# Placing zero rows, sums, first tokens and expert outputs differently in a graph transformer layer on one core

## What is computed

```python
x = x + gnn(xn, src, dst, edge_attr_20, edge_weight, edge_attr_3) + linear_attention_block(xn)
x = x + moe(layernorm(x))
# gnn: 40,000 edges from idx_j to idx_i
h   = softplus(f_ij @ Wf1 + bf1) - log 2
W   = (h @ Wf2 + bf2) * rcut_ij[:, None]
agg = segment_sum(message(xn[idx_j], direction of r_ij, W), idx_i, 1250)   # 8 x 128 numbers a node
# moe: 8 experts, hidden 1024, each token goes to its best two
out = sum over e of dense_w[:, e] * ((silu(z @ w_gate[e]) * (z @ w_up[e])) @ w_down[e])
```

## Time and profile before

| | before |
|---|---|
| three runs, median | 1680.25 us (1678.17 to 1683.88) |
| the profiled execution, its own time | 1677.54 us |
| its span in the profile | 1675.8 us |
| mean granted TensorE clock | 0.927 of full speed |
| busy: PE, DVE, ACT, POOL | 1448.5, 852.4, 636.9, 759.3 us |
| front block | 0 to about 452 us (last record scatter), next block's first work at 463.2 us |
| edge block | to about 1027 us |
| block of the sums | 1033.7 to 1069.5 us |
| node block | to about 1134 us |
| expert block | to 1675.8 us |

### The profile page before, as it was taken

How to read it: one execution, slowest core, us unless ns; L and a number is a source line. 1 busy time by engine, 2 the same in 40 slices (tenths; PEclk the granted TensorE clock), 3 DMA queues, 4 the chain that set the end, 5 groups by cost and what they waited for, 6 DMA issues and landing times. The chain is left out here.

```text
span 1675.8 us, 29431 instructions
## 1 busy us (share of the span) xinstructions
PE 1448.5 (86%) x8631; PEld 893.0 (53%) x8632; DVE 852.4 (51%) x1980; ACT 636.9 (38%) x1191; POOL 759.3 (45%) x783
## 2 busy tenths in 40 slices
PE   6466998777369999999999996678999999999995
PEld 3243454344124444444444443377787877887784
DVE  7745665577437777777777776452111111111111
ACT  2354555544226666666666664420100110000010
POOL 4577777777635655556565562006211111111111
PEclk7787999898679999999999998777999999999998
DMA  6665333332268888888888888531154252354113
GB/s 260 223 203 157 112 115 115 117 115 106 84 185 246 250 249 248 251 244 251 242 253 251 247 243 231 195 113 19 25 176 144 56 175 79 121 172 172 20 24 80
DMA packets 130911, 275.35 MB, mean 164 GB/s; under 512 B 21286, under 2 KB 68090, under 8 KB 129906
## 3 DMA queue, kind: packets, MB, share of 16 engines
q0 software_dynamic: 50432, 151.03, 30.5%
q1 hardware_dynamic: 80354, 121.25, 21.8%
q10 hardware_dynamic: 80, 2.56, 0.5%
HBM read 211.81 MB, written 65.50 MB: 165 GB/s over the span
## 5 line engine op out<-in xcount | busy, mean ns | idle before, releaser
L1048 POOL DMA_INDIRECT shared<-node_table,shared x343 | 324.2, 945 | 245.5 <-DVE msg L1116 144.6
L1608 PEld LDWEIGHTS psum<-zT,shared 128*128 128x128 f32 x2944 | 349.9, 193 | 66.6 <-issue 64.1
L1608 PE MATMUL psum<-zT,shared 128*128 128x128 f32 x2944 | 353.9, 276 | 9.1 <-issue 5.8
L394 POOL DMA_INDIRECT edge_list<-rec,place x313 | 311.4, 995 | 108.8 <-issue 94.7
L1118 DVE TENSOR_TENSOR msg<-shared,psum 128x768 f32<-128x768 f32 x339 | 321.2, 948 | 0.0
L1144 PE MATMUL psum<-wf,hT 128*128 128x512 f32 x678 | 315.3, 608 | 3.9 <-ACT psum L1080 3.9
L1080 ACT COPY psum<-bias 128x512 f32<-128x512 f32 x343 | 202.1, 590 | 194.6 <-DVE msg L1118 187.6
L1626 ACT ACTIVATE sg<-psum 128x128 f32<-128x128 f32 x184 | 51.0, 277 | 466.7 <-PE psum L1608 466.7
L1116 DVE TENSOR_TENSOR msg<-shared,psum 128x256 f32<-128x256 f32 x339 | 141.0, 416 | 148.9 <-PE psum L1144 147.4
L1672 DVE TENSOR_TENSOR hid<-sg,psum 128x128 f32<-128x128 f32 x184 | 52.6, 286 | 321.4 <-ACT sg L1626 321.4
L1144 PEld LDWEIGHTS psum<-wf,hT 128*128 128x128 f32 x678 | 122.3, 190 | 162.4 <-issue 144.0
(11 more groups left out here) (278 smaller groups left out, 1486.1 us busy)
## 6 DMA issues: line engine op xcount, KB each, us to landing
shared<-edge_list SPq DMA_DIRECT2D x356, 130.0 KB
shared<-in_L_ffn_w_gate SPq DMA_DIRECT2D x8, 2048.0 KB, 9.4
shared<-in_L_ffn_w_up SPq DMA_DIRECT2D x8, 2048.0 KB, 14.3
shared<-in_L_ffn_w_down SPq DMA_DIRECT2D x8, 2048.0 KB, 18.9
shared<-node_table,shared POOLq DMA_INDIRECT x343, 3.7
edge_list<-rec,place POOLq DMA_INDIRECT x313, 2.6
raw<-in_records SPq DMA_DIRECT2D x19, 256.0 KB, 3.5
xrow<-in_x SPq DMA_DIRECT2D x10, 250.0 KB
```

The source lines that it names most:

```text
L394: nc.gpsimd.indirect_dma_start(out=edge_list, out_offset=bass.IndirectOffsetOnAxis(ap=place[:n_, c:c + 1].bitcast(U32), axis=0), in_=rec[: ...
L1048: nc.gpsimd.indirect_dma_start(out=gat[:, k % G, :], out_offset=None, in_=table, in_offset=bass.IndirectOffsetOnAxis(ap=ix, axis=0)).then_ ...
L1608: ins = nc.tensor.matmul(GU[m % 2][:, o:o + BLK], w[u][:, j, m * P:(m + 1) * P], zT[:, j, :], start=(j == 0), stop=(j == DJ - 1))
```

## The change

Four edits. (1) The three large zero scatters are no longer written ahead of the records, but one each after the record scatters of stages 3, 5 and 7; the five small ones stay in front. (2) In the block of the sums, DVE subtracts groups 4 to 9 (group 4 first, into a spare area `low`), POOL subtracts groups 3 to 1. All register loads of the offsets are taken out of the copy loop: ACT does its 40 before its first copy, DVE does four after each of its subtractions and 12 before its first copy. The second half of the last group is placed by ACT in place of DVE. (3) The token numbers are split into two parts that bf16 holds exactly, `pick` is written in bf16, and each one-column product becomes two bf16 products. (4) The down products are copied by ACT from PSUM to `yraw`, which frees the bank; the multiplication by the token's weight (`gate`) is done by DVE from `yraw` at m = 5 of the next block, and after the last block. POOL's add-scatter waits for `gated`.

```diff
-        tok_f = sb("tok_f", [P, NC_])
+        tok_b = sb("tok_b", [P, NC_, 2], BF16)
...
+            CLEAR_AT = {3 + 2 * d: d for d in range(ZG)}
...
-                    for d in range(ZI):
+
+                    def clear_rows(d):
                         src_, dst_ = (zeros, edge_list.rearrange("(g a) r -> g (a r)", a=GR)) if d < ZG else (zeros[:, 0:RECW], edge_list)
                         nc.gpsimd.indirect_dma_start(out=dst_, out_offset=bass.IndirectOffsetOnAxis(ap=zero_at[:, d:d + 1].bitcast(U32), axis=0),
                                                      in_=src_, in_offset=None).then_inc(zeroed, 16)
+
+                    for d in range(ZG, ZI):
+                        clear_rows(d)
                     for u in range(NQ):
                         if u == 0:
                             pool.wait_ge(placed_cols, 1)
...
                             nc.gpsimd.indirect_dma_start(
                                 out=edge_list, out_offset=bass.IndirectOffsetOnAxis(ap=place[:n_, c:c + 1].bitcast(U32), axis=0),
                                 in_=rec[:n_, u % 3, j, :], in_offset=None).then_inc(placed[u % 3], 16)
+                        if u in CLEAR_AT:
+                            clear_rows(CLEAR_AT[u])
                     pool.wait_ge(zeroed, 16 * ZI)
                     for i in range(3):
...
-                def place_sums(eng, copy, i, g, half_, done):
+                HALF_G = 4
+                low = shared[:, NG * 8 * P:(NG + 1) * 8 * P]
+
+                def offsets(eng, groups):
+                    return {(g, j): eng.value_load(perm[0:1, g * TS + j:g * TS + j + 1], min_val=0, max_val=NB - 1) for g in groups for j in range(TS)}
+
+                def place_sums(copy, at, i, g, half_, done):
                     src = bank[i % 4 * 2 + half_][:].rearrange("p (c j w) -> p c w j", c=4, j=TS)
                     for j in range(TS):
-                        b = eng.value_load(perm[0:1, g * TS + j:g * TS + j + 1], min_val=0, max_val=NB - 1)
-                        ins = copy(aggT[:].rearrange("p c (w b) -> p c w b", b=NB)[:, half_ * 4:half_ * 4 + 4, :, bass.ds(b, 1)], src[:, :, :, j:j + 1])
+                        ins = copy(aggT[:].rearrange("p c (w b) -> p c w b", b=NB)[:, half_ * 4:half_ * 4 + 4, :, bass.ds(at[g, j], 1)], src[:, :, :, j:j + 1])
                     ins.then_inc(done, 1)
...
                     a, b = float(2 * P) ** -0.5, float(P) ** -0.5
-                    for g in reversed(range(1, NG)):
-                        nc.vector.tensor_tensor(agg[:, g, :], agg[:, g, :], agg[:, g - 1, :], ALU.subtract).then_inc(parted, 1)
+                    at = {}
+                    for g in (HALF_G, *reversed(range(HALF_G + 1, NG))):
+                        nc.vector.tensor_tensor(agg[:, g, :] if g > HALF_G else low, agg[:, g, :], agg[:, g - 1, :], ALU.subtract).then_inc(parted, 1)
+                        at.update(offsets(dve, (g,)))
...
                     nc.vector.tensor_scalar(w2[:], w2[:], b, None, ALU.mult).then_inc(w_scaled, 1)
-                    for i, g in enumerate(reversed(range(NG))):
+                    at.update(offsets(dve, range(1, HALF_G)))
+                    for i, g in enumerate(reversed(range(1, NG))):
                         dve.wait_ge(agg_turned, i + 1)
-                        place_sums(dve, nc.vector.tensor_copy, i, g, 1, placed_b)
+                        place_sums(nc.vector.tensor_copy, at, i, g, 1, placed_b)
+                @block.gpsimd
+                def _(pool):
+
+                    pool.wait_ge(parted, 1)
+                    for g in reversed(range(1, HALF_G)):
+                        nc.gpsimd.tensor_tensor(agg[:, g, :], agg[:, g, :], agg[:, g - 1, :], ALU.subtract).then_inc(parted_low, 1)
                 @block.tensor
                 def _(pe):
                     for i, g in enumerate(reversed(range(NG))):
-                        pe.wait_ge(parted, min(i + 1, NG - 1))
+                        if g >= HALF_G:
+                            pe.wait_ge(parted, min(NG - g + 1, NG - HALF_G))
+                        else:
+                            pe.wait_ge(parted_low, HALF_G - max(g, 1))
                         if i >= 4:
                             pe.wait_ge(placed_a, i - 3)
                             pe.wait_ge(placed_b, i - 3)
                         for c in range(8):
-                            ins = nc.tensor.transpose(psum[:, (i % 4) * 1024 + c * P:(i % 4) * 1024 + (c + 1) * P], agg[:, g, c * P:(c + 1) * P], ident)
+                            ins = nc.tensor.transpose(psum[:, (i % 4) * 1024 + c * P:(i % 4) * 1024 + (c + 1) * P], (low if g == HALF_G else agg[:, g, :])[:, c * P:(c + 1) * P], ident)
                         ins.then_inc(agg_turned, 1)
 
                 @block.scalar
                 def _(act):
+                    at = offsets(act, reversed(range(NG)))
                     for i, g in enumerate(reversed(range(NG))):
                         act.wait_ge(agg_turned, i + 1)
-                        place_sums(act, nc.scalar.copy, i, g, 0, placed_a)
+                        place_sums(nc.scalar.copy, at, i, g, 0, placed_a)
+                    place_sums(nc.scalar.copy, at, NG - 1, 0, 1, placed_b)
...
                         dve.wait_ge(tok_in, 16)
-                        nc.vector.tensor_copy(tok_f[:CR, :], tok[:CR, :])
+                        nc.vector.tensor_scalar(tok_2[:CR, :, 0], tok[:CR, :], 0xFFE0, None, ALU.bitwise_and)
+                        link(nc.vector.tensor_scalar(tok_2[:CR, :, 1], tok[:CR, :], 0x1F, None, ALU.bitwise_and))
+                        nc.vector.tensor_copy(tok_b[:CR], tok_2[:CR])
...
+            pick = sbi("pick", [P, 2, NC_, P], BF16)
...
+            yraw = sbi("yraw", [P, D])
+            GATE_AT = 5
...
                     def give(waited):
-                        wait_alone(pool, y_bank, waited)
+                        wait_alone(pool, gated, waited)
                         nc.gpsimd.indirect_dma_start(out=acc, out_offset=bass.IndirectOffsetOnAxis(ap=to[:, 0:1].bitcast(U32), axis=0),
                                                      in_=yo[:], in_offset=None, compute_op=ALU.add).then_inc(y_out, 16)
...
                         for c in range(NC_):
                             if c % (NC_ // 2) == 0:
                                 pe.wait_ge(picked_s, 2 * n_ + 1 + c // (NC_ // 2))
-                            ins = nc.tensor.matmul(bank[5 + n_][:, 0:1], pick[:CR, n_, c, :], tok_f[:CR, c:c + 1], start=(c == 0), stop=(c == NC_ - 1))
+                            for k in range(2):
+                                ins = nc.tensor.matmul(bank[5 + n_][:, 0:1], pick[:CR, n_, c, :], tok_b[:CR, c, k:k + 1],
+                                                       start=(c == 0 and k == 0), stop=(c == NC_ - 1 and k == 1))
                         ins.then_inc(ids_mm, 1)
...
                     nb = n_blocks(act)
                     nc.scalar.activation(rstd[:CR, :], rstd[:CR, :], ACT.Silu)
+                    act.sem_inc(y_bank, 1)
+                    act.sem_inc(gated, 1)
                     with act.Fori(0, nb) as b:
                         for m in range(HM):
                             act.wait_ge(gu_mm, b * HM + (m + 1))
                             nc.scalar.activation(sg[:, m % 4, :], GU[m % 2][:, 0:BLK], ACT.Silu).then_inc(silu_done, 1)
+                        act.wait_ge(y_mm, b + 1)
+                        act.wait_ge(gated, b + 1)
+                        nc.scalar.copy(yraw[:], bank[4][:]).then_inc(y_bank, 1)
                     wait_alone(act, y_out, nb * 16 + LISTED)
                     flat = lambda a: a.rearrange("n d -> (n d)").rearrange("(a b) -> a b", a=80)
                     act.dma_start(flat(out), flat(acc[0:N, :])).then_inc(stored, 16)
...
-                    dve.sem_inc(y_bank, 1)
...
-                    with dve.Fori(0, nb) as b:
+
+                    def gate(b):
+                        dve.wait_ge(y_bank, b + 2)
+                        dve.wait_ge(y_out, b * 16 + LISTED)
+                        dve.wait_ge(to_in, b * 16 + 16)
+                        nc.vector.tensor_scalar(yo[:], yraw[:], to[:, 1:2], None, ALU.mult).then_inc(gated, 1)
+
+                    def block_(b, last):
                         for m in range(HM):
                             if m == HM - 1:
 
                                 dve.wait_ge(gu_mm, b * HM + HM)
                                 copy_turned(b + 3)
+                            if m == GATE_AT and last is not None:
+                                gate(last)
                             dve.wait_ge(silu_done, b * HM + (m + 1))
                             nc.vector.tensor_tensor(hid[:, m, :], sg[:, m % 4, :], GU[m % 2][:, BLK:2 * BLK], ALU.mult).then_inc(hid_slots, 1)
-                        dve.wait_ge(y_mm, b + 1)
-
-                        dve.wait_ge(y_out, b * 16 + LISTED)
-                        dve.wait_ge(to_in, b * 16 + 16)
```

(11 more changed lines are left out.)

4 lines of the change are left out of this document (2 added, 2 removed).

## The result

| | median, us | range, us | runs |
|---|---|---|---|
| before | 1681.9 | 1678.17 to 1683.88 | 4 |
| changed | 1665.36 | 1659.4 to 1666.39 | 4 |

The ratio is 0.9891, with a 95% interval of 0.9871 to 0.9911: 16.5 us or 1.0% to 1.1% faster, where 9.1 us (0.5%) were forecast. Timed again on another chip it was 1665.31 us against 1682.8 us, ratio 0.9895 (0.9876 to 0.9914). The profiled execution of the changed kernel took 1665.34 us, span 1663.6 us. The direction was right and the median lies inside the range of 1664 to 1679 us, near its fast end. Set against the 1680.25 us that the forecast started from, the same gain gives 1663.7 us by the medians and 1661.9 us by the ratio, just outside it. The change is worth nearly twice the forecast.

The account below looks back on a forecast made before the run. PE was taken to bound the edge and steady expert blocks, POOL's issue the front. Front -5.2, sums -0.9, first tokens and gate -3.0 made -9.1: 1680.25 to 1671.2 us, range 1664 to 1679.

Parts of the forecast that it names:

- The step that failed: Front block: POOL's issue sets the pace, 1.265 us a scatter, and the block ends when everything is issued.
- the sum of edit 1: Front block: earlier start 0.5 and hole 10.7 gained, moved scatters 3.8 back, new stall 2.2: -5.2 us.
- The hole: Front block: POOL's 11.02 us idle ahead of stage 2's scatters shrinks to the usual 0.30, gain 10.7 us.
- DVE in order of time tells why: Front block: POOL idled 11.02 us because DVE's statistics waited 13.89 us for `xrow`, with `record(2)` behind them.
- The stall at group 3: Front block: group 3's load comes at 74.1 behind two zero writes, so POOL starts stage 8 2.2 us late.
- the lower bound: Front block: no new stall before stage 8 (0 instead of 2.2 us), since loads get part of the engines during zero writes.
- The rival in which each zero write holds the records for 16.6 us: Front block: large zero writes delay record scatters, stalling POOL 18.0 us; sum +6.7, 1686.9 us; chance 0.09.
- a sign of being wrong: Front block: DVE's records waiting for `placed` in stages 7 to 11 would show the forecast wrong.
- The sums: Block of the sums: loads first, ACT's 44 copies 0.30 us apart, 13.2 us, end at 1068.6 instead of 1069.49: -0.9 us.
- the forecast's lower bound of -2.7: Block of the sums: ACT's copies only 0.26 us apart, as on DVE, would give -2.7 us.
- First tokens: First-token products in bf16: result moves from 1141.31 to 1139.95, behind DVE's second `pick`: -1.4 us, bounds 0 and -2.7.
- the gate: Expert block: PE's 2.29 us wait in the second block goes, -2.3 us; ACT's copy and handover at the end, +0.7.

Follow-up runs that it names:

- the edit alone: Kernel before with only one of the four edits: zero rows 1672.63 us, sums 1677.94, first tokens 1681.0, gate 1677.81.
- edit 4: Kernel before with only the gate change (expert outputs copied by ACT, gated in the middle of the next block): 1677.81 us, ratio 0.9967.
- edit 2: Kernel before with only the sums change (subtractions parted by DVE and POOL, register loads ahead of the copies): 1677.94 us, ratio 0.9967.
- edit 1: Kernel before with only the three large zero scatters moved behind the record scatters of stages 3, 5 and 7: 1672.63 us, ratio 0.9934.
- the parts 2, 3 and 4: Kernel before with one change each: sums 1677.94 us, first tokens in bf16 1681.0, gate 1677.81.
- the three later kernels that hold edit 1: Changed kernel with offsets loaded at the front's end, 1662.5 us; spread over the front, 1656.57; spread and no subtraction on GpSimd, 1652.46.
- Two experiments: Kernel before with statistics two stages later, 1677.14 us; kernel before with small zero writes first and sixteen semaphore increments on ScalarE, 1673.19 us.

## Why it came out as it did

| stretch | forecast | before | changed, again | the edit alone |
|---|---|---|---|---|
| last record scatter at | -5.2 | 451.3 | 447.9, 447.0 | 447.4 |
| POOL's drain | none | 7.99 | 5.38, 5.38 | 5.38 |
| edge block, first to next block's first work | none | 570.6 | 572.5, 573.7 | |
| block of the sums | -0.9 | 36.0 | 34.8, 34.5 | 34.2 |
| node block, to the slots | none | 65.5 | 64.1, 64.1 | 64.3 (edit 4) |
| slots to first turned block | -1.4 | 11.2 | 9.6, 9.5 | 9.5 |
| to the last `yo` | -1.6, both rows | 510.2 | 508.8, 508.5 | 509.2 |
| last `yo` to output copy | | 6.7 | 6.1, 6.2 | 6.2 |
| output copy to end | none | 12.3 | 10.7, 10.6 | 10.5 (edit 4), 10.9 (edit 2) |

**The step that failed** is in the first part of the prediction, "the front block ends when POOL has issued everything": it puts the drain behind POOL's last issue at nothing, and with it the sum of edit 1 is too small. The block ends when POOL has drained, and that is 2.6 us sooner with a zero write moved. On top the last record moved by somewhat more than 5.2 us: the profile of before that the forecast worked with has the earliest last record of four old fronts (451.3; the parts 2, 3 and 4 have 454.5, 454.9 and 453.8). Against their mean of 453.6 the first three new ones (447.4, 447.9 and 447.0) are 6.2 us earlier; with the three later kernels that hold edit 1 (447.6, 446.1 and 450.3) it is 5.9. So edit 1 is -8.8 us by the profiles, and by its timing -7 to -15, not -5.2. What the drain hangs on is half open: it is 7.992 us in all six profiles with the eight writes in front of the records, in either order, and 5.379 us in all ten with two, three or eight of them behind. Why was not found.

That step is the largest of several. Of the 8.8 us by which the stretches below exceed the forecast of 9.1, the drain is 2.6 and the last record 1.0. The issue of the output copy, a row that the forecast left out, is 1.7. The way from the first turned block to the output copy, with the clock behind PE's stall, is 1.5. The node block is 1.2, the sums 0.6 and the first tokens 0.2.

**The hole.** It went as forecast, but "DVE in order of time tells why" was only half the cause. Two waits ended within a microsecond of each other, one at `xrow`, at 50.19 us, and one at the landing of the first quad. The list of waits shows only the one in front, but the trace of before has the other too, in the landing of the quad's last scatter, issued at 36.3 us and so landed at 50.0:

```profile
L394 POOL DMA_INDIRECT edge_list<-rec,place x1: 960/960/960, 36.3 to 36.3; - x1
...
DMA to landing us min/median/max: 13.7/13.7/13.7
```

Two experiments took the first away and met the second, 11.07 and 8.14 us. The forecast's size was right by luck: moving the zero writes removes both, and only one had been seen.

**The stall at group 3** did not come. It was taken at 2.2 us since the loads were thought to stand still during zero writes; group 3 was used at 69.14 us with no wait, not at 74. `wk` was issued at 44.10 us, and by the forecast's own 18.7 us group 3 would come at 62.8 without zero writes, and at 67.8 if the loads stood still for the first one. It landed at 65.4, while that write was in flight from 52.87 to 64.9. So the loads went on beside it at a lower pace. That speaks for the lower bound, and agrees with what the Trainium skill (DMA: Bandwidth & Descriptors, Queues, rings and completion order) says of a DMA engine alternating between queue rows. POOL was nonetheless at stage 8 at 78.04 us where 76.3 was free of stalls and 78.5 forecast: the 1.7 us came from scatters whose issue took 1.05 to 1.45 us instead of 0.96; every profile has 45 to 59 such scatters of 313. The rival in which each zero write holds the records for 16.6 us fell: the writes landed in at most 12.0 us, and DVE waited at most 3.6 us there, POOL not at all. Such waits of the records had been named as a sign of being wrong; they came, and POOL's queued work hid them.

**The sums.** -0.9 was forecast, -1.2 to -1.8 measured. The loads run 0.53 us apart on ScalarE, 21.5 us, as the sum has them; a load itself takes 0.275 us in the median. The trace disagrees with the floor of about 600 ns that the Trainium skill gives (DMA: Bandwidth & Descriptors, Latency and other measured facts). ScalarE's copies are 0.26 us apart, as in the forecast's lower bound of -2.7, but two waits for PE gave most of that back: 13.0 us for the 44 copies, where the forecast had 13.2. GpSimd's subtractions, 2.97 us each, had their cover; that they slow VectorE's down was not seen, and was hidden behind the loads too. A rule that the forecast had passed over bears on these rows: the Trainium skill (SBUF — State Buffer, Who interferes with whom) says that a VectorE instruction with two SBUF inputs contends with a GpSimd instruction that reads SBUF. Both engines' subtractions are of this kind, and the trace agrees, with 1.15 us alone and 2.23 in the mean beside GpSimd.

**First tokens** were right at -1.6 for -1.4, **the gate** in its mechanism. Its stall had a second price that the forecast lacked, the fall of PE's clock, in five of the seven profiles without edit 4 on the faster chips. At the end ScalarE's copy puts `yo` 0.82 us back (1646.02 to 1646.84), and from there to the output copy it is 0.5 us shorter, the gate out of SBUF taking 0.49 us for 0.75 out of PSUM: +0.3 for the +0.7. The node block, in which nothing was changed, has two lengths too: 63.9 to 64.3 us in six profiles, five with edit 4 and one without it, and 65.1 to 65.7 us in ten, three of them with edit 4. So its 1.2 us are not shown to belong to the edit, and stay open.

**The output copy,** -1.7 us, is no property of an edit: a fetch falls on this instruction or not. Edits 2 and 4 each shift ScalarE's program and each get the gain alone, but it can be had once. That is one reason why the parts add up to more than the whole; the intervals of the parts, 5 to 8 us wide, leave room for the rest.

Added up against typical profiles of before: -6.2 - 2.6 - 1.5 - 1.2 - 1.6 - 2.6 (508.9 against 511.5, the means of four and seven profiles) - 0.5 - 1.7 = -17.9 us, in the order of the table's other rows. The edge block, which no edit touches, is 570.6 to 573.3 us in six profiles of the old front (572.1 in the mean) and 572.5 and 573.7 in the changed kernel, so it takes about 1 us of this back: -16.9, where -16.5 and -17.5 were measured.

## What to carry to other kernels

A wait that the trace shows hides those that would have ended just before it: ask what the engine reaches next and when that lands (the landing times are in the trace), before a hole is put down to one cause. The end of a block is the end of its last drain, and the start of the next block is the row to measure from, not the last useful instruction. Loads of registers cost half a microsecond each here and need nothing but their source: off the path they were worth 8 to 9 us (ratios of 0.9895 and 0.9843), behind the last stage of a block only 2.8. A part timed alone can carry a gain that is no property of it, as the output copy's issue shows: compare rows by stretch before adding parts up.

## What had not been expected of the hardware

- The issue of one DMA takes 0.63 us or 2.4 to 2.6 us, by whether a packet of the instruction queue falls into it (six profiles with, ten without); sixteen semaphore increments ahead changed it.
- POOL's closing drain of the front block has two lengths, 7.992 us in six profiles and 5.379 us in ten, the same to the nanosecond. The ten include three on the chip whose front and edge blocks ran slower.
- Three 128x1024 subtractions on GpSimd (2.97 to 3.3 us each) slow VectorE's from 1.15 to 2.23 us in the mean: nine on VectorE alone take 10.3 us, six beside GpSimd's three 13.4.
- PE waits of 2.44 to 2.68 us in the second expert block were followed by a fall to a mean granted clock of 0.57 to 0.65 over four microseconds in five profiles; behind waits of 1.84 and 2.29 us at the same place, in two others, it stayed at 1.00.
- One chip took 1814.44 us for the kernel that took 1682 to 1684 on three others; kernels of two calls can't be compared by their medians in us, only each with the kernel before of its own call.
